# The second mixture of experts: every token through all experts, against tokens sent to their two experts, with the shared expert behind the next group's router logits

## The reference, cut to what matters

```python
def _L1_ffn_ref(x, gate_w, experts_gate_up, experts_down, shared_gate_w, shared_up_w, shared_down_w, shared_expert_gate_w):
    HIDDEN_SIZE = 128
    NUM_EXPERTS = 8
    MOE_INTERMEDIATE_SIZE = 176
    NUM_EXPERTS_PER_TOK = 2
    SHARED_EXPERT_INTERMEDIATE_SIZE = 352
    ...
    logits = x_flat @ gate_w.T
    scores = jax.nn.softmax(logits, axis=-1)
    _, topk_ids = jax.lax.top_k(scores, NUM_EXPERTS_PER_TOK)
    in_topk = jax.nn.one_hot(topk_ids, E, dtype=x.dtype).sum(axis=1)
    w = scores * in_topk
    gu = jnp.einsum('nh,eih->nei', x_flat, experts_gate_up)
    g, u = (gu[..., :I], gu[..., I:])
    h = jax.nn.silu(g) * u
    expert_out = jnp.einsum('nei,ehi->neh', h, experts_down)
    out = jnp.einsum('neh,ne->nh', expert_out, w)
    shared = jax.nn.silu(x_flat @ shared_gate_w.T) * (x_flat @ shared_up_w.T) @ shared_down_w.T
    shared_weight = jax.nn.sigmoid(x_flat @ shared_expert_gate_w.T)
    out = out + shared_weight * shared
```

## Time and profile before

| | |
|---|---|
| three runs | 2123.80, 2124.75, 2131.32 us (median 2124.75) |
| profiled execution, its own time | 2112.62 us |
| its span in the trace | 2110.8 us |
| PE busy | 1813.6 us, 86% of the span |
| first dense stage (902.3 to 1223.9) and its lead-in from 877.6 | 346.3 us |
| latent attention (1223.9 to 1768.2) | 544.3 us |
| second dense stage (1768.2 to 2101.7) | 333.5 us |
| store of the result (2101.7 to 2110.8) | 9.1 us |

### The profile page before, as it was taken

How to read it: one execution, slowest core, us unless ns; L and a number is a source line. 1 busy time by engine, 2 the same in 40 slices (tenths; PEclk the granted TensorE clock), 3 DMA queues, 4 the chain that set the end, 5 groups by cost and what they waited for, 6 DMA issues and landing times.

```text
span 2110.8 us, 38449 instructions
## 1 busy us (share of the span) xinstructions
PE 1813.6 (86%) x10812; PEld 1379.7 (65%) x10813; DVE 1239.8 (59%) x4206; ACT 689.7 (33%) x1279; POOL 584.9 (28%) x946
## 2 busy tenths in 40 slices
PE   3758994899844699299999969999999998999998
PEld 2547992555533699289988955555555555988987
DVE  2555885555545588566666555665655652556654
ACT  0114551222200355122232214444444442232222
POOL 2652675566257366532211010000000000000000
PEclk9758996999855799699999969999999998999999
DMA  5111212000001121100000000000000000000001
GB/s 200 38 43 51 60 50 93 25 20 21 3 29 45 57 60 55 55 21 12 19 11 11 1 0 1 1 0 0 0 0 0 0 0 1 1 0 0 0 1 41
DMA packets 61796, 54.18 MB, mean 26 GB/s; under 512 B 8579, under 2 KB 55044, under 8 KB 61189
## 3 DMA queue, kind: packets, MB, share of 16 engines
q1 hardware_dynamic: 52070, 34.20, 5.3%
q0 software_dynamic: 8192, 16.79, 2.7%
q10 hardware_dynamic: 1440, 2.10, 0.3%
HBM read 31.56 MB, written 21.50 MB: 25 GB/s over the span
## 4 chain that ended last, share of the span: by engine, by line
PE 70%; POOL 10%; DVE 8%; issue 8%; DMA 2%; SPq 1%; POOLq 1%; ACT 1%; DVEq 1%; ACTq 0%
PE bk L1007 14%; PE bk L1664 10%; PE bk L582 6%; PE bk L990 5%; PE bk L992 5%; PE bk L991 5%; POOL xs L368 4%; PE bk L1652 3%; PE bk L575 3%; PE bk L1639 2%; PE bk L1590 2%; PE bk L564 2%; PE bk L565 2%; PE bk L566 2%; DMA sb_X<-x 1%
## 5 line engine op out<-in xcount | busy, mean ns | idle before, releaser
L1007 PEld LDWEIGHTS bk<-sb_wd,sb_sc 128*128 128x128 f32 (+1 forms) x2688 | 333.0, 192 | 23.2 <-DVE sb_X L1106 3.6
L1007 PE MATMUL bk<-sb_wd,sb_sc 128*128 128x128 f32 (+1 forms) x2688 | 336.7, 275 | 0.0
L1092 DVE TENSOR_TENSOR sb_sc<-sb_sb_,bk 128x512 f32<-128x512 f32 x224 | 152.2, 684 | 230.4 <-PE bk L992 220.2
L112 POOL TENSOR_TENSOR sb_ln_ve<-sb_ln_mv,sb_eps 128x2 f32<-128x2 f32 (+1 forms) x48 | 9.4, 195 | 998.9 <-DVE sb_ln_mv L104 998.9
L1046 ACT ACTIVATE sb_sb_<-bk 128x512 f32<-128x512 f32 x224 | 133.8, 598 | 444.8 <-PE bk L992 442.0
L1918 DVE TENSOR_REDUCE sb_sc<-bk 128x2 f32<-128x512 f32 x256 | 164.6, 688 | 157.0 <-PE bk L1639 153.0
L1664 PE MATMUL bk<-sb_sa,sb_sb_ 128*32 128x256 f32 x1024 | 249.1, 387 | 0.7 <-ACT sb_sc L1813 0.7
L1826 ACT ACTIVATE sb_sa<-bk 128x512 f32<-128x512 f32 x256 | 151.1, 597 | 185.0 <-PE bk L1652 184.9
L1106 DVE SCALAR_TENSOR_TENSOR sb_X<-bk,sb_gate,sb_X 128x128 f32 (+1 forms) x576 | 161.4, 342 | 4.2 <-PE bk L1007 1.8
L582 PE MATMUL bk<-sb_w2c,sb_sb_ 128*128 x1152 | 152.2, 275 | 0.0
L368 POOL DMA_INDIRECT xs<-sb_xn,sb_send_row x128 | 128.7, 1006 | 80.3 <-DVE sb_send_row L357 44.0
(11 more groups left out here) (284 smaller groups left out, 3427.4 us busy)
## 6 DMA issues: line engine op xcount, KB each, us to landing
sb_sc<-xs SPq DMA_DIRECT2D x144, 64.0 KB, 1.9
ys<-sb_sc SPq DMA_DIRECT2D x36, 256.0 KB, 2.3
xs<-sb_xn,sb_send_row POOLq DMA_INDIRECT x128, 2.2
out<-sb_X SPq DMA_DIRECT2D x1, 2048.0 KB, 8.7
sb_sa<-w SPq DMA_DIRECT2D x1, 1792.0 KB, 14.2
sb_sc<-w SPq DMA_DIRECT2D x1, 1792.0 KB, 17.5
sb_sa<-w_gu SPq DMA_DIRECT2D x1, 1760.0 KB, 6.8
xs<-sb_zeros SPq DMA_DIRECT2D x24, 64.0 KB, 1.6
```

Of the source, the lines that this page charges most:

```text
L1007: ins = pe.matmul(bank[:, j * P:(j + 1) * P], p.hT[0:m, c % HRING, j * P:(j + 1) * P], p.wd[0:m, q * D:(q + 1) * D], start=(c == FIRST[e] ...
L1092: dve.tensor_tensor(p.hT[0:m, c % HRING, :], p.sg[0:m, c % 2, :], p.bk[2 + c % 2][0:m, :], ALU.mult)\
```

## The change

Both "swiglu" blocks are routed like the first mixture, and the shared expert is computed in the routing part. New names: `sr_` routing part, `sh_` shared expert, `se_` expert part.

Routing part. Per group PE issues the rank of group g, the transposes and logits of group g+1, and then all shared-expert work of group g: three chunks of six matmuls of 512 columns (`sh_up_pe`, the last chunk 96 rows) and 12 down matmuls of 128 columns (`sh_down_pe`, f32). POOL scatters rows that are 132 wide (the token's number and its first expert travel with it) to `xs2`. In the first sweep the gathers for the preceding block are issued three groups ahead.

Expert part. Each of 18 units takes, per tile, three matmuls of 352 columns with the tokens as the stationary side, silu and product of 128x176, two transposes, and two down matmuls; DVE copies the unit's 128x512 result (`se_out_dve`), and POOL scatters it with four indirect transfers to `y2`, where each of a token's two results has a fixed place (`se_back_pool`). SP loads four slot tiles for each unit.

Adding. Nothing is gathered afterwards: the next block loads `y2` with plain transfers, two of 256 KB for each group. In "mla" they are added with 8 DVE instructions per group ahead of the statistics (`at_combine_dve`), one group every second element. Behind the second sweep stands a new block "out", which loads, adds and stores group by group; the single store at the end is gone. Buffers are laid over the weights of the first mixture, which is over by then (`sb_w1l` in the rows below is `xq`, the normalized rows, or `sw_yo`, the unit's result), and the rows of zeros are loaded and no longer set.

```diff
-def sw_pe_group(pe, p, g, par, last):
-    for c in range(2, NCH):
-        sw_gu(pe, p, g, c, par)
-        sw_down(pe, p, g, c - 2)
-        if c == 7 and not last:
-            pe.wait_ge(p.rt2.sem, p.rt2.at(7 * g + 7))
-            x_transpose(pe, p, g + 1, p.xf, p.bk[6])
-        if c == 10 and not last:
-            router_logits(pe, p, g + 1, 1 - par, p.bk[6], p.wr1h[:], p.wr1l[:], NL)
-    for c in range(2):
-        if not last:
-            sw_gu(pe, p, g + 1, c, 1 - par)
-        sw_down(pe, p, g, NCH - 2 + c)
...
+def sh_up_pe(pe, p, g, c, par):
+    n, m, q = NSC * g + c, shared_rows(c), (par + c) % 2
+    for at, bank, done, freed in ((SHARED, p.bk[q], p.sh_g, p.sh_s), (SHARED + SI, p.bk[2 + q], p.sh_u, p.sh_h)):
+        rows = slice(at + c * P, at + c * P + m)
         if not isinstance(n, int) or n >= 2:
             pe.wait_ge(freed.sem, freed.at(n - 1))
+        pe.matmul(bank[0:m, :], p.wguh[:, rows], p.xh[:, par, :], start=True, stop=False)
+        pe.matmul(bank[0:m, :], p.wgul[:, rows], p.xh[:, par, :], start=False, stop=False)
+        pe.matmul(bank[0:m, :], p.wguh[:, rows], p.xl[:, par, :], start=False, stop=True).then_inc(done.sem, 1)
+def sh_down_pe(pe, p, g):
+    pe.wait_ge(p.sh_h.sem, p.sh_h.at(NSC * (g + 1)))
+    pe.wait_ge(p.sh_add.sem, p.sh_add.at(TG * g))
+    for j in range(TG):
+        for c in range(NSC):
+            m = shared_rows(c)
+            ins = pe.matmul(p.bk[7][:, j * P:(j + 1) * P], p.sh_hT[0:m, c, j * P:(j + 1) * P],
+                            p.wd[0:m, DOWN + c * D:DOWN + (c + 1) * D], start=(c == 0), stop=(c == NSC - 1))
+    ins.then_inc(p.sh_d.sem, 1)
...
+def sr_pe_group(pe, p, g, par, last=False):
+    route_rank_pe(pe, p, g)
+    if not last:
+        sr_x_pe(pe, p, g + 1, 1 - par)
+        sr_logits_pe(pe, p, g + 1, 1 - par)
+    for c in range(NSC):
+        sh_up_pe(pe, p, g, c, par)
+    sh_down_pe(pe, p, g)
...
+def sr_dve_group(dve, p, g, par, after, first=False, ahead=2):
+    route_top_dve(dve, p, g, NL)
+    route_rows_dve(dve, p, g, par, sr_carry_dve)
+    if ahead >= 1:
+        route_apply_dve(dve, p, g + 1, 1 - par, p.xq, P, first)
+    if ahead >= 1:
+        sr_x_dve(dve, p, g + 1, 1 - par)
+    for c in range(NSC):
+        sh_product_dve(dve, p, g, c, par)
+    if ahead >= 2:
+        if after:
+            sr_combine_dve(dve, p, g + 2, par)
+        route_stats_dve(dve, p, g + 2, par)
+    route_weights_dve(dve, p, g, E)
+    sh_add_dve(dve, p, g)
+def sr_pool_group(pool, p, g, par, after, ahead=3):
+    route_send_pool(pool, p, g, par, p.xq, p.xs2)
+    if ahead >= 2:
+        route_scale_pool(pool, p, g + 2, par)
+    if ahead >= 3 and after:
+        combine_ahead_pool(pool, p, g + 3, 1 - par)
...
+def se_pe_unit(pe, p, k, par, ahead=3):
+    word = sw_word(pe, p, k)
+    e = [expert_of(word, n) for n in range(2 * TG)]
+    for half in range(2):
+        if ahead >= 1:
+            for j in range(2 * half, 2 * half + 2):
+                se_up_pe(pe, p, k + 1, 1 - par, e[TG + j], j)
+        if half == 0:
+            se_turn_pe(pe, p, k, 1)
+        elif ahead >= 1:
+            se_turn_pe(pe, p, k + 1, 0)
+        se_down_pe(pe, p, k, par, half, e[2 * half:2 * half + 2])
+    if ahead >= 3:
+        se_x_pe(pe, p, k + 3, 1 - par)
...
+def se_back_pool(pool, p, k, par):
+    pool.wait_ge(p.slot_of.sem, p.slot_of.at(4 * k + 4))
+    if not isinstance(k, int) or k >= 2:
+        pool.wait_ge(p.back[par].sem, p.back[par].at(32 * (k - par)))
+    pool.sem_inc(p.pool_passed.sem, 1)
+    pool.tensor_copy(p.slot_send[:, par, :], p.slot_row[:, bass.ds(k * TG, TG)]).then_inc(p.slot_to.sem, 1)
+    pool.wait_ge(p.slot_to.sem, p.slot_to.at(k + 1))
+    pool.wait_ge(p.se_y.sem, p.se_y.at(k + 1))
+    pool.sem_inc(p.pool_passed.sem, 1)
+    for j in range(TG):
+        pool.indirect_dma_start(p.y2, bass.IndirectOffsetOnAxis(ap=p.slot_send[:, par, j:j + 1], axis=0),
+                                p.sw_yo[:, par, j, :], None).then_inc(p.back[par].sem, 16)
...
+def out_sp(sp, p, out):
+    back_wait_sp(sp, p)
+    for g in range(NG):
+        back_load_sp(sp, p, g, p.out_taken, OUT_RING, p.bgot[g % 2])
+        if g >= OUT_RING - 1:
+            out_store_sp(sp, p, g - OUT_RING + 1, out)
+    for g in range(NG - OUT_RING + 1, NG):
+        out_store_sp(sp, p, g, out)
+def out_store_sp(sp, p, g, out):
+    sp.wait_ge(p.bcomb.sem, p.bcomb.at(TOP * TG * (g + 1)))
+    sp.dma_start(out[:, g * TG:(g + 1) * TG, :], tiles(p, g)).then_inc(p.stored.sem, 16)
...
+def out_dve(dve, p):
+    for g in range(NG):
+        dve.wait_ge(p.bgot[g % 2].sem, p.bgot[g % 2].at(16 * TOP * (g // 2 + 1)))
+        back_combine_dve(dve, p, g, p.out_taken[g % OUT_RING])
...
 def at_dve(dve, p):
+    at_combine_dve(dve, p, 0)
     for b in range(2):
         ln_stats(dve, p, b, NB2)
         ln_apply(dve, p, b, p.xn[:, 0], P - 1, NB2)
+    at_combine_dve(dve, p, 1)
...
-PHASES = ["moe", "gau", "moe", "swiglu", "mla", "swiglu"]
+PHASES = ["moe", "gau", "moe", "swiglu", "mla", "swiglu", "out"]
```

More of the change, by code:

```diff
@@ L966 @@
 I1, SI = 176, 352
[L967 to L987 removed]
+GU = 2 * I1
@@ new lines, in se_pe @@
+def se_pe(pe, p):
+    se_x_pe(pe, p, 0, 0)
+    se_x_pe(pe, p, 1, 1)
+    pe.wait_ge(p.fin.sem, p.fin.at(NFIN))
+    word = sw_word(pe, p, 0)
+    for j in range(TG):
+        se_up_pe(pe, p, 0, 0, expert_of(word, j), j)
+    se_x_pe(pe, p, 2, 0)
+    se_turn_pe(pe, p, 0, 0)
+    se_pe_unit(pe, p, 0, 0)
+    se_pe_unit(pe, p, 1, 1)
+    with pe.Fori(1, UNITS // 2 - 2) as i:
+        se_pe_unit(pe, p, 2 * i, 0)
+        se_pe_unit(pe, p, 2 * i + 1, 1)
+    for k in range(UNITS - 4, UNITS):
+        se_pe_unit(pe, p, k, k % 2, ahead=UNITS - 1 - k)
@@ new lines, in se_out_dve, with se_dve_unit @@
+def se_out_dve(dve, p, k, par):
+    dve.wait_ge(p.se_o.sem, p.se_o.at(2 * k + 2))
+    if not isinstance(k, int) or k >= 2:
+        dve.wait_ge(p.back[par].sem, p.back[par].at(32 * (k - par)))
+    dve.tensor_copy(flat(p.sw_yo[:, par]), p.bk[4 if par == 0 else 7][:]).then_inc(p.se_y.sem, 1)
+def se_dve_unit(dve, p, k, par, ahead=3, behind=True):
+    for half in range(2):
+        if ahead >= 1:
+            for j in range(2 * half, 2 * half + 2):
+                se_product_dve(dve, p, k + 1, j)
+        if half == 0 and behind:
+            se_out_dve(dve, p, k - 1, 1 - par)
+    if ahead >= 3:
+        se_x_dve(dve, p, k + 3, 1 - par)
@@ new lines, in se_dve @@
+def se_dve(dve, p):
+    for k in range(2):
+        se_x_dve(dve, p, k, k)
+    for j in range(TG):
+        se_product_dve(dve, p, 0, j)
+    se_x_dve(dve, p, 2, 0)
+    se_dve_unit(dve, p, 0, 0, behind=False)
+    se_dve_unit(dve, p, 1, 1)
+    with dve.Fori(1, UNITS // 2 - 2) as i:
+        se_dve_unit(dve, p, 2 * i, 0)
+        se_dve_unit(dve, p, 2 * i + 1, 1)
+    for k in range(UNITS - 4, UNITS):
+        se_dve_unit(dve, p, k, k % 2, ahead=UNITS - 1 - k)
+    se_out_dve(dve, p, UNITS - 1, 1)
@@ new lines, in sw_pool @@
+    for g in range(2):
+        route_scale_pool(pool, p, g, g)
+    if after:
+        combine_ahead_pool(pool, p, 2, 0)
+    sr_pool_group(pool, p, 0, 0, after)
+    sr_pool_group(pool, p, 1, 1, after)
+    with pool.Fori(1, NG // 2 - 2) as i:
+        sr_pool_group(pool, p, 2 * i, 0, after)
+        sr_pool_group(pool, p, 2 * i + 1, 1, after)
+    for g in range(NG - 4, NG):
+        sr_pool_group(pool, p, g, g % 2, after, ahead=NG - 1 - g)
+    for k in range(2):
+        se_back_pool(pool, p, k, k)
```

605 lines of the change are left out of this document (343 added, 262 removed).

## The result

The changed kernel takes 2289.03 us (median of four runs, 2281.59 to 2291.99) against 2127.07 of the kernel before (2123.80 to 2131.32): ratio 1.0755, interval 1.072 to 1.0789. Slower was forecast, at 2213 and within 2150 to 2275; the time lies above that range. The profiled execution took 2291.99 us, with a span of 2290.2.

The account below looks back on a forecast made before the run. PE was taken to bound the kernel before; the change trades full PE stages for waits. Stage terms +42.1, +5, +17.4 and +23.4 gave +88 on the median 2124.75, so 2213 us, range 2150 to 2275.

Parts of the forecast that it names:

- The routing parts: Both routed stages: lead-ins of 34.3 and 10 us, eight groups of 196.7 in the first sweep and 183.5 in the second.
- the way to the first scatter: From the last routing group to a unit's first scatter, at the lower clock: 38 us in each sweep.
- the attention stage: Latent attention, where the first block's results are added back: +5 us, to 549.3; +20 if each second element were fully delayed.
- "out": New last block, 4 MB in and 2 MB out: 32.5 us against 9.1, or 20 if the transfers overlap better.
- 18 x 6.35 = 114: Expert part: POOL's copy and four transfers take 6.35 us a unit against PE's 5.4, for 18 units a sweep.
- The first sweep's group: First routing sweep: nearly one chain of PE and DVE, 26.2 us a group.
- POOL's 22.4: First routing sweep: POOL's 16 indirect transfers, a scale and a copy per group, 22.4 us beside the PE and DVE chain.
- the sum: Whole kernel: first routed stage +42.1, attention +5, second routed stage +17.4, "out" +23.4, together +88 us.
- The two drains: POOL's drain behind each sweep's units, before the next stage: 5.4 us each.
- the lower level: Rival for the expert units: PE at the lower clock, 10 us a unit, binds; +126 us, 2339; chance 0.05.
- the rival of PE at the upper clock through them: Routing groups: PE at the upper clock, 4.4 us less a group, 71 in all, 2142; chance 0.06.
- The rival on the other side: Routing groups: each costs its fullest engine, POOL's 22.4 or PE's 17; 86 us less, 2127; chance 0.09.

Follow-up runs that it names:

- the run without the delay: The changed kernel itself, unedited, run again in a later set of runs on one chip: 2165.11 us against 2289.03 before.
- the version with both orders: Changed kernel with shared chunks between the router's steps on PE, and adds and statistics of group g+2 ahead of the last two products: 2098.57, later 2101.12 us.
- the fourth set: Earlier files run again on one chip, kernel before at 2113.46: changed kernel 2165.11, both orders 2101.12, store and four scatters 2170.92, plain store 2130.25 us.
- the second set: Changed kernel with SP's plain store, way back left out, other POOL work beside it: memsets 2187.12, two scatters 2191.42, four scatters 2263.20, four gathers 2270.63 us.
- the third: Changed kernel with DVE's combine and statistics earlier 2152.2, both orders 2098.57, plain store with three scatters 2156.13 us; kernel before at 2112.25.

## Why the prediction was wrong

- **The direction and its reason were right.** The change gives up stages in which PE is full at 2.4 GHz for stages full of waits. The routing parts, the way to the first scatter, the attention stage and "out" came as forecast, within 4 us each, but for the first sweep's groups.
- **The step that failed** is in the expert part: "So POOL's transfers bind, not PE: 18 x 6.35 = 114". In the profiled execution neither binds. A unit took 8.1, with POOL standing up to 5.12 us for DVE, because PE's signals to ACT and DVE came late while POOL's transfers were under way: 78 of 190 by over 1 us, the latest by 7.4. The forecast had no rival of this kind: every wait in it ended when the producer did. Two sweeps of that are 64 of the 91 us of the miss.
- **The first sweep's group** (26.2 forecast, 31 measured) failed by the same delay, which closed a ring through POOL's sixteen transfers. The experiment without gathers opened it (24.5 to 26.9), as did the run without the delay (24.5 to 26.9). The forecast had POOL's 22.4 "beside this"; the ring is POOL's 22.4 plus the 8 us that it stood for the DVE steps behind a late product, and it cost 25 us in the sweep.
- **Where signals come in time**, the mechanisms hold and sizes are off by little: the changed kernel is 51.7 us slower than the kernel before (2165.11 - 2113.46), where the sum said 88, and POOL does bind the units. Its 2165.11 would lie within the stated range, so whether the forecast was met hung on a condition that it did not know. Units at 5.8 from copy to copy and not 6.35 give 21 of the difference (10.9 + 10.4): I had counted 0.30 behind the fourth transfer, which is there only between two transfers, and 0.2 for register work that is hidden. The groups were 0.8 us too dear in the first sweep (25.4 on average) and 0.5 in the second, together 9.5 with the last ones; the ways to the first scatter 4. The two drains, 9.3 and 6.7 us, were 5.2 too cheap together.
- **The clock.** Units were granted 0.99 and not the lower level, as forecast; under the delay 0.85, with longer stretches in which PE stood. The routing groups were granted 0.65 to 0.70, a mix of both levels, so the rival of PE at the upper clock through them did not occur. The Trainium skill, "TensorE: Matmul & The Clock Gate", Part 4, says that a transpose does not count as PE being busy in the way a matmul does. In this unit 12 of 40 records are transposes, and the 0.99 shows that they did not bring the clock down.
- **The rival on the other side** ("the shared expert is hidden after all", 0.09) did not occur in this kernel, for the reason given: the next top two stands behind the add. Its price rule, a group costs what its fullest engine does, came true in the version with both orders in the first sweep, where POOL ran through (22.5 for 22.4). In the second sweep the number came out as well (17.3 for PE's 17), but not for that reason: PE was busy 12.9 us of the 17.3 (90.01 for seven groups), so that agreement is luck. The version gained 64 us (2165.11 to 2101.12), where the rival had 86.

What each order is worth without the delay: the combine ahead of the products about 12 us (2152.2, one execution, is 39.95 above its kernel before, the changed kernel 51.65), the shared chunks between the router's steps 54 more (2152.2 to 2098.57), part of it by the higher granted clock.

**What stays open.** Why PE's signals come late in some executions is not settled. The runs show this much:

- It goes with the number of indirect transfers that POOL issues in a unit (none 5.4, two 5.7 to 5.9, four 7.5 to 7.9 us), not with their direction, not with POOL's being busy, not with the row size and not with slower transfers. Two thirds of the late signals come as POOL's last transfer lands.
- It is there for the same program in one set of runs and not in another. It is not a matter of the chip alone: the second set had it, and the third, on the same chip, did not. It moves the kernel before only by 0.6% (2127.07 against 2113.46).
- The traces of such runs lack records of signals.

The ends of PE's matmuls in a trace are modelled, so no run here separates a signal that is held from a result that is finished late; PE itself goes on meanwhile (its next matmul starts at 1234.49, the signal of the transposes comes at 1237.36). The missing records may mean that the recording and the signals share a way, but that is argued and no run here separates them. The Trainium skill, "NOTIFIC — the notification-queue block", section 7.1, says that the block that writes such records can drop them when a ring is full, and that its internal pipeline holds its producers back rather than lose one. Were that so here, an execution without recording would be free of the delay, which no run here shows.

The profiled execution of before was one without the delay, so its trace could not warn: none of its signals was over 0.1 us late, and it has 10,842 records of signals in its first 870 us, about as many as the 10,991 of the changed kernel in the fourth set, where the changed kernel's first trace has 8,677. Its time, 2112.62, also agrees with the 2113.46 of that set and not with the 2123.80 to 2131.32 of the executions beside it.

## What to carry to other kernels

Before costing a ring of short steps through several engines, look at whether the profiled execution belongs to the same population as the timed ones: here it was 0.57% faster than their median, and that was the only sign of a condition that costs the changed kernel 6% (2289.03 against 2165.11). What was exposed to it here is a stage in which POOL issues four indirect transfers per 5.4 us of matmul work, with short waits on PE's results; the kernel before, most of which is long stretches of matmuls, moved 0.6%. And a routed part comes near what its fullest engine costs only if independent work stands between the dependent steps in each engine's order: the same instructions took 25.4 or 21.3 us a group with the order changed, and 23.5 or 17.3 where the granted clock rose with it.

## What the runs showed of the hardware

- The same program took 2289.03 or 2165.11 us, while the kernel before moved from 2127.07 to 2113.46. Under the slower condition ACT took up PE's result 2.66 and 4.55 us late, otherwise 0.03.
- Under the slower condition 100 of PE's 1,913 recorded signals were over 1 us late, up to 7.4 us, and none of 5,862 of ACT, DVE and POOL; of 98 late ones, 67 came 1.8 to 2.5 us after the start of POOL's last indirect transfer, and such a transfer lands 2.2 to 2.3 us after its issue.
- An indirect transfer on POOL holds it 0.96 us with 0.30 until the next one; another instruction behind it starts with no gap (1170.38 + 0.96 = 1171.34).
- From POOL's last scatter to the next stage 9.3 us went by before "mla" (from 1240.7 to 1250.0) and 6.7 before "out" (from 2126.4 to 2133.1); behind plain arithmetic on POOL it had been 5.66.
